# Fewer matmuls for the squared norms: sums on VectorE, squares of the output weights on ScalarE

## The reference, cut to what matters

```python
def _rfs(xw, ab, AB, gs):
    dot_products = einsum('...d,rd->...r', xw, ab[:, None] * gs)
    correction = (0.5 * sum(xw * xw, axis=-1))[..., None] * (ab * ab)
    return 1.0 / sqrt(1024) * AB * exp(dot_products - correction)

weights = _rfs(input_weights, xis, exp(xis), proj_matrix)     # [1024 outputs, 1024 features]
feats   = _rfs(x, xis, exp(xis), proj_matrix)                 # [tokens, 1024 features]
x = layernorm(x + einsum('bsr,or->bso', feats, weights))
gate, up = x @ wg.T, x @ wu.T                                 # 3072 hidden, int8 weights / 127
x = layernorm(x + (silu(gate) * up) @ wd.T)
```

## Time and profile before

| | us |
|---|---|
| median of 3 runs (lowest) | 631.32 (630.61) |
| profiled execution | 631.02 |
| its span, slowest core (core 4) | 629.5 |
| spans of all cores | 625.6 to 629.5 |
| TensorE busy | 594.1 (94%) |
| VectorE busy | 426.7 (68%) |
| GpSimd busy | 382.0 (61%) |
| ScalarE busy | 197.0 (31%) |

### The profile page before, as it was taken

How to read it: one execution, slowest core, us unless ns; L and a number is a source line. 1 busy time by engine, 2 the same in 40 slices (tenths; PEclk the granted TensorE clock), 3 DMA queues, 4 the chain that set the end, 5 groups by cost and what they waited for, 6 DMA issues and landing times.

```text
span 629.5 us, 9280 instructions; the slowest of 8 cores (625.6 to 629.5 us)
## 1 busy us (share of the span) xinstructions
PE 594.1 (94%) x2776; PEld 271.6 (43%) x2832; DVE 426.7 (68%) x681; ACT 197.0 (31%) x368; POOL 382.0 (61%) x345
## 2 busy tenths in 40 slices
PE   3699999999979899999999999999999999999994
PEld 1244444455534344444444444444444444444442
DVE  1275933555867877777778777777777857886765
ACT  0244424466672222322322232232230013310243
POOL 9201999300004546999999999999813596624940
PEclk9999999999998999999999999999999999999998
DMA  8999261655410011134224224133431928865433
GB/s 99 163 170 268 94 223 36 201 201 189 147 51 0 2 67 68 35 125 139 75 105 160 77 84 157 50 113 133 165 130 51 317 101 300 300 218 207 179 134 135
DMA packets 28194, 86.08 MB, mean 137 GB/s; under 512 B 2416, under 2 KB 9584, under 8 KB 24816
## 3 DMA queue, kind: packets, MB, share of 16 engines
q1 hardware_dynamic: 19696, 54.54, 24.8%
q0 software_dynamic: 8448, 30.94, 19.0%
HBM read 60.82 MB, written 23.59 MB: 134 GB/s over the span
## 4 chain that ended last, share of the span: by engine, by line
PE 81%; DVE 5%; ACT 5%; issue 5%; DMA 3%; POOL 1%; DVEq 0%; ACTq 0%; POOLq 0%
PE P L550 44%; PE P L814 22%; PE P L299 8%; PE P L331 4%; DVE z L464 3%; DMA proj<-projT 3%; ACT junk L434 2%; PE P L263 1%; ACT lnst L435 1%; PE P L364 1%; PE P L446 1%; DVE xsum L189 1%; ACT lnst L437 0%; ACT junk L732 0%; POOL xf L80 0%
## 5 line engine op out<-in xcount | busy, mean ns | idle before, releaser
L550 PE MATMUL P<-x1t,ring 128*128 128x512 bf16 x751 | 181.3, 381 | 4.0 <-DVE ebuf L569 2.1
L550 PE MATMUL P<-xsum,ring 128*128 128x512 bf16 x565 | 140.5, 383 | 4.0 <-ACT x1t L505 3.4
L189 POOL TENSOR_TENSOR ring<-ring 128x512 bf16<-128x512 bf16 x120 | 135.1, 1158 | 13.1 <-DMA ring<-wgu 9.3
L550 PEld LDWEIGHTS P<-x1t,ring 128*128 128x128 bf16 x768 | 75.1, 98 | 94.8 <-issue 6.5
L611 POOL TENSOR_TENSOR hact<-wbuf,hact 128x512 bf16<-128x512 f32 x24 | 27.8, 1160 | 115.7 <-DVE wbuf L608 114.4
L189 POOL TENSOR_TENSOR stage<-stage 128x512 bf16<-128x512 bf16 x60 | 70.8, 1215 | 44.0 <-DMA stage<-wd 42.1
L550 PEld LDWEIGHTS P<-xsum,ring 128*128 128x128 bf16 x576 | 56.5, 98 | 72.6 <-issue 6.0
L814 PE MATMUL P<-tbuf,hact 128*128 128x512 bf16 x376 | 83.3, 379 | 0.4
L299 PE MATMUL P<-xf,proj 128*128 128x512 bf16 x252 | 58.3, 387 | 16.6 <-DMA proj<-projT 14.9
L814 PE MATMUL P<-tbuf,sbuf 128*128 128x512 bf16 x283 | 62.5, 379 | 0.3
L565 ACT ACTIVATE ebuf<-P 128x512 f32<-128x512 f32 x48 | 28.2, 588 | 100.0 <-PE P L550 100.0
(11 more groups left out here) (84 smaller groups left out, 690.2 us busy)
## 6 DMA issues: line engine op xcount, KB each, us to landing
tbuf<-t_hbm SPq DMA_DIRECT2D x14, 1536.0 KB, 8.3
ring<-wgu POOLq DMA_DIRECT2D x12, 1024.0 KB, 5.1
xtok_sb<-xtok SPq DMA_DIRECT2D x16, 512.0 KB, 3.6
t_hbm<-stage SPq DMA_DIRECT2D x8, 896.0 KB, 5.1
stage<-wd POOLq DMA_DIRECT2D x12, 512.0 KB, 3.6
xf<-xfm POOLq DMA_DIRECT2D x16, 256.0 KB, 25.4
x_hbm<-x1k SPq DMA_DIRECT2D x16, 256.0 KB, 2.0
xres<-x_hbm SPq DMA_DIRECT2D x16, 256.0 KB, 6.9
```

Of the source, the lines that this page charges most:

```text
L189: out[o] = (p.mark(eng, lambda e, c=c: e.tensor_tensor(d[:, c:c + step], a[:, c:c + step], b[:, c:c + step], op), *toks, *behind),)
L550: fn = lambda e, dk=dk, lhsT=lhsT, rhs=rhs: e.matmul(bank(b), lhsT, rhs, start=(start and dk == 0), stop=(stop and dk == 3), skip_group_ch ...
```

## The change

The squares of a tile are added up on VectorE before the matmuls: after each square of 128x2048 (4 chunks) one add of 128x1024, and one more add of 128x1024 over the two halves, so 2 chunks are left and 2 matmuls do what 8 did. The squares of the output weights go from VectorE to ScalarE (one each after the exponentials of unit (1,1) and (2,0), two after (2,1)), and `add_w` folds them in six adds on VectorE, two chunks of 1024 columns are left, and 4 matmuls do what 16 did; these now stand inside `w_unit(0)` ahead of dk 6 instead of behind it. The ten ring sums of slot 1 go from GpSimd to VectorE, five behind `w_evict(1)` and five behind `w_evict(2)`.

```diff
-    def ring_sums(n, w):
-        w_sum[n, w] = sums(lambda i: slot_block(n % 2, i, w * 512, w * 512 + 512), (ld_ring[n],), ["gpsimd"] * 5)
+    def ring_sums(n, w, eng="gpsimd"):
+        w_sum[n, w] = sums(lambda i: slot_block(n % 2, i, w * 512, w * 512 + 512), (ld_ring[n],), [eng] * 5)
...
     def norm_x(t):
         o = (t % 2) * 4096
+        half = []
         for k in range(2):
             a, b = k * 2048, (k + 1) * 2048
-            t_sq[t, k] = p.mark("vector", lambda e, a=a, b=b: e.tensor_tensor(
+            t_q = p.mark("vector", lambda e, a=a, b=b: e.tensor_tensor(
                 sqx[:, o + a:o + b], xf[:, t * 4096 + a:t * 4096 + b], xf[:, t * 4096 + a:t * 4096 + b], OP.mult),
                 ld_x[t, 2 * k], ld_x[t, 2 * k + 1], sq_read.get(t - 2))
+            half.append(p.mark("vector", lambda e, c=o + a: e.tensor_tensor(
+                sqx[:, c:c + 1024], sqx[:, c:c + 1024], sqx[:, c + 1024:c + 2048], OP.add), t_q))
+        t_sq[t] = p.mark("vector", lambda e: e.tensor_tensor(
+            sqx[:, o:o + 1024], sqx[:, o:o + 1024], sqx[:, o + 2048:o + 3072], OP.add), *half)
...
     def norm_x_mm(t, b):
         o = (t % 2) * 4096
-        for dk in range(DK):
...
+        p.run("tensor", lambda e: e.matmul(bank(b), mhalf[:, :], sqx[:, o:o + 512], start=True, stop=False),
+              t_sq[t], t_half, freed[b])
+        sq_read[t] = p.mark("tensor", lambda e: e.matmul(
+            bank(b), mhalf[:, :], sqx[:, o + 512:o + 1024], start=False, stop=True))
...
     def norm_w(k):
         a, b = k * 2048, (k + 1) * 2048
+        t_sq["w", k] = p.mark("scalar", lambda e: e.activation(sqw[:, a:b], iw[:, a:b], AF.Square), ld_iw[k])
+
+    def add_w(k, far):
+        c = k * 2048
+        toks = (t_sq["w", k], t_sq["w", k + 1] if far == 2048 else None)
         t_sq["w", k] = p.mark("vector", lambda e: e.tensor_tensor(
-            sqw[:, a:b], iw[:, a:b], iw[:, a:b], OP.mult), ld_iw[k])
+            sqw[:, c:c + 1024], sqw[:, c:c + 1024], sqw[:, c + far:c + far + 1024], OP.add), *toks)
...
@@ w_unit
         for dk in range(DK):
+            if dk == 6 and mid is not None:
+                mid((b0 + 4) % 8 + 2)
...
-        if mid is not None:
-            mid((b0 + 4) % 8 + 2)
...
@@ norm_w_mm
-        for dk in range(DK):
+        for k in (0, 2):
             for h in range(2):
...
+                fn = lambda e, c=k * 2048 + h * 512, h=h, k=k: e.matmul(
+                    bank(b + h), mhalf[:, :], sqw[:, c:c + 512], start=(k == 0), stop=(k == 2))
...
     feat_evict(1, 1, *u)
+    norm_w(0)
     u = feat_unit(2, 0, mid=lambda b: norm_x_mm(2, b))
     feat_evict(2, 0, *u)
-    norm_w(0)
     norm_w(1)
+    add_w(0, 1024)
     u = feat_unit(2, 1)
     feat_evict(2, 1, *u)
     norm_w(2)
     norm_w(3)
+    add_w(1, 1024)
+    add_w(0, 2048)
     u = feat_unit(3, 0, mid=lambda b: norm_x_mm(3, b))
     feat_evict(3, 0, *u)
+    for w in (2, 3):
+        add_w(w, 1024)
+    add_w(2, 2048)
     for n in range(4):
         u = w_unit(n, mid=norm_w_mm if n == 0 else None)
...
         w_evict(n, *u)
+        if n in (1, 2):
+            ring_sums(1, n - 1, "vector")
...
     for n in range(2):
-        for w in range(2):
-            ring_sums(n, w)
+        if n == 0:
+            for w in range(2):
+                ring_sums(0, w)
         stage_load(n + 2)
```

More of the change, by code:

```diff
@@ L361, in norm_w_mm @@
     def norm_w_mm(b):
-        for dk in range(DK):
+        for k in (0, 2):
             for h in range(2):
[L364 to L368, removed]
+                fn = lambda e, c=k * 2048 + h * 512, h=h, k=k: e.matmul(
+                    bank(b + h), mhalf[:, :], sqw[:, c:c + 512], start=(k == 0), stop=(k == 2))
+                if k == 0 or h == 0:
+                    p.run("tensor", fn, t_sq["w", k], freed[b + h])
                 else:
```

## The result

The change made the kernel slower: 636.08 us (median of 6 runs, 633.74 to 636.89) against 632.25 (6 runs), ratio 1.0067, 95% interval 1.0056 to 1.0079, so about 4.2 us. (Two of the six runs of before, at 653 to 655 us, were disturbed; the ratio leaves them out.) The forecast was 629.3, with a range up to 632.6: wrong in its direction.

A forecast was written before the change was run, and what follows sets the result against it. TensorE was taken as the bound, VectorE nearly as tight. Gain 8.6 - 2.7 (tile 1) - 1.3 (tile 2) - 2.7 (weights) = 1.9, by the steps 2.0, giving 629.3 us; range 626.4 to 632.6.

The forecast's parts named there:

- Matmuls removed, VectorE the bound in tiles 1 and 2: Token and weights' norms: 36 matmuls fewer, 7.8 us, ceiling 8.6; VectorE's queue cancels the gain in tiles 1 and 2.
- Add of 128x1024: VectorE's fold of the squares: 0.69 us each, split from the 1.23 us square of 128x2048.
- Square on ScalarE: Weights' squares of 2048 columns after the exponentials: 1.9 us each, bounds 1.06 and 2.12, hidden.
- Part 4: Three weights' adds behind eviction (3,0), slowed by GpSimd: TensorE waits 2.7 us, can be 0.4 to 5.6; gain 2.0 us.
- rival 2: Weights' adds hardly meet GpSimd, its earlier store pause falls on them: wait 0.4 us, gain 4.3, 627.0 us; chance 0.20.
- The surcharge of 0.9 us: Weights' adds beside GpSimd's sums: 0.69 + 0.9 = 1.6 us each, from the median stretched square of 2.11 us.
- rival 4: TensorE's clock falls in the new wait before the weights' norm matmuls: gain 2.0 - 1.8, 631.1 us; chance 0.12.
- rival 5: One of the last three weights' adds is held 3.8 us: wait 5.6 us, clock falls too, 634.2 us; chance 0.12.
- Its sign: For rival 5, at the weights' adds: an add starts while GpSimd issues its store, as the 5.00 us square did.
- Ring sums: Ten adds of 128x512 on VectorE before weight evictions: 2.1 to 6.5 us per five, cost nothing, up to 4 us uncovered.
- GpSimd's 11.7 us gained: GpSimd loses 11.7 us of ring-sum work but waits 89 us for gate and up anyway: no gain.
- a wait of at most one instruction: Weights' adds under the skill's rule: each waits one GpSimd instruction of 1.16 us at most, 1.85 us each, gain 0.9.

The follow-up runs named there:

- The reordering: On the kernel with GpSimd late: eviction (0,1) moved between tile 1's two squares, tile 3's squares moved behind eviction (1,1); ratio to before 0.9979.
- the weights alone: Only the weights' part put in the kernel before: squares on ScalarE, six adds, 4 norm matmuls ahead of dk 6; 636.8 us, ratio 1.0060.
- the kernel with GpSimd late: The changed kernel with GpSimd's down-weight sums waiting for the weights' last norm matmul; ratio to before 1.0018.
- the kernel with the pause: The changed kernel with only GpSimd's first ring sums waiting for the weights' norm matmuls, down-weight sums as early as in the change; 629.8 us, ratio 0.9948.

## Why the prediction was wrong

Each step as a distance from the first norm matmul (23.92 in the forecast, 23.75 on core 7), forecast and measured: norm of tile 1 16.8 and 17.2; of tile 2 32.4 and 33.1; of tile 3 46.7 and 47.4; third weights' norm matmul 57.2 and 60.0; second half of tile 3's features 80.1 (83.25 and 96 matmuls at 0.216) and 85.6.

- **Matmuls removed, VectorE the bound in tiles 1 and 2**: right. In tile 1 the wait for bank 7 was 2.86 us on core 7, for a forecast of 2.68. The wait before tile 2, forecast at 1.25, stands on five cores with 1.15 and not on core 7, where the clock had fallen in between. The reordering shows that the queue's order was the cause. The 0.7 us by which these steps are off are clock in tile 2's stretch and data that came at a slightly different time.
- **Add of 128x1024**: 0.69 forecast and measured. **Square on ScalarE**: 1.9 forecast, 1.90 measured; hidden but for 0.20 us before the fourth matmul of `w_unit(0)`, which waits for the copy of tile 3's norm and which the forecast had missed.
- **The weights' adds, the step that failed (Part 4)**: priced at 1.6, 1.6 and about 1 us, they took 3.1, 1.6 and 1.5. The forecast let GpSimd's pause around its store fall on the third add and took it for a cheap place. The store is the dear place. A two-input instruction of VectorE that starts once the store's issue has begun is held until the third sum behind it has ended. On all eight cores the first of the three adds started 1.5 to 1.9 us after the issue had begun, and was held for 2.3 to 2.7 us. GpSimd had come to its second store sooner than before (75.60 on core 7, 77.47 on core 4 before), as rival 2 had said. At the old place it would have been no better: by the forecast's own times the second add starts at about 78.2, inside the issue from 77.47 to 78.39. The surcharge of 0.9 us, the median of the earlier trace rows, is right for sums that have no store right ahead of them. That is 1.7 us more in the three adds, 2.1 in the step.
- **The clock, the second half of the failure**: it was rival 4, priced at 1.8 us and given 0.12, on the ground that a wait of 2.7 us lay on the edge. With a wait of 4.2 to 5.5 us it fell on every core: 2.7 us in this step on core 7. The two belong together, since a longer add is a longer wait, and rival 5 said so (634.2 us, 0.12). Its mechanism came true, with 4.34 us of wait instead of 5.6. Only its sign, an add that starts while GpSimd issues its store, was too narrow: the three sums behind the store hold one as well.
- **Ring sums**: priced at nothing; alone they measured nothing (1.0002). In the change they cost 0.4 us before attention, because the later evictions had less room.
- **GpSimd's 11.7 us gained are worth nothing**: right. The 89 us of the earlier trace rows are several waits added up; the first, before gate and up, is 79.8 us on core 4, which changes nothing here. The other direction was not asked: that more work late would collide with the layernorms.

Forecast -2.0 us, measured about +4.2: 2.1 (adds), 2.7 (clock), 0.7 (tiles 1 and 2), 0.4 (attention) make 5.9 of the 6.2 between them; the rest is not accounted for. The parts are those of core 7, the slowest of the profiled execution.

The Trainium skill (SBUF — State Buffer, on the shared port pair) says that a VectorE instruction with two SBUF inputs and a GpSimd instruction exclude each other for the whole instruction. The experiments agree with the exclusion: 6.23 us with GpSimd streaming, 2.08 without, for the same three adds. They do not agree with a wait of at most one instruction, which the prediction had drawn from it: the first add took 3.12 us instead of 0.69 beside sums that record 1.3 us each, and the one-column instruction 4.18 instead of 0.16.

## What to carry to other kernels

Before moving sums to VectorE, look at what GpSimd does at that very time, and above all where it issues a store and goes on with sums. A two-input VectorE instruction that starts there waited for three sums to end, however small it was; beside other sums it lost 1.0 us at most. The 12 matmuls saved on the weights are 2.6 us, and TensorE lost 4.3 us to the wait and 2.4 to the clock behind it. Leaving the last fold out, or holding GpSimd back for just the few microseconds of the adds, turned +0.7% into -0.5%. When a producer is put ahead of an eviction in an in-order queue, check who needs it first: moving it behind the eviction gave another 0.3 to 0.4%.

## What the runs showed of the hardware that was not expected

- What a two-input VectorE instruction loses behind a GpSimd store goes by when it starts, and not by its size. In the traces of this case 178 of VectorE's squares, adds, ring sums and one-column instructions were held for over 1.8 us within the first 200 us. All of them started 0.1 to 2.4 us after GpSimd began to issue a store to `t_hbm`, and all ended behind the third sum that followed it, some 4.3 us after that beginning. So a start 0.2 us behind it costs 4.0 us (the single column, and 128x512 ring sums), 0.4 us behind costs 3.8 (the 128x2048 square), 1.8 us behind costs 2.4 (the add at 77.36). Beside sums without a store right ahead of them no such instruction lost more than 1.0 us. Whether it is the store or the way the three sums follow each other behind it (they start 1.11 us apart) is open: no run takes the store away.
- The length of a wait alone does not say whether the clock falls. Behind waits of 3.8 to 5.5 us before the third weights' norm matmul it fell on all 24 cores of the three kernels that have them (the change, the weights alone, the change without the ring sums). In tile 1 it fell behind 2.10 us on core 6 of the kernel with GpSimd late (granted clock 0.50 from 42 to 44 us), and not behind 3.37 us on core 7 of the kernel with the pause (1.00 from 38 to 46 us).
- 22 useless matmuls in a wait made the program 0.5% faster than the idle wait.
